# Window attention with token-major output, row sums from a ones column, and bias matmuls in 64-column tiles

## What is computed

```python
x = x + conv_ref(ln_c(x))                 # window attention, with residual
t = tokens(x);  t = t + ffn(ln_t(t))      # experts, with residual

# conv_ref, per window of 49 tokens
qkv  = xw @ w_qkv.T + b_qkv
attn = einsum('qd,kd->qk', q, k) / sqrt(8) + bias + mask
p    = softmax(attn, axis=-1)
o    = einsum('qk,kd->qd', p, v)
out  = o @ w_proj.T + b_proj

# ffn
probs = softmax(x @ gate_w + gate_b); masked = top-2 of probs, divided by their sum
y = sum_e masked[e] * (gelu(x @ w1[e] + b1[e]) @ w2[e] + b2[e])
```

## Time and profile before

| | |
|---|---|
| median of 3 runs | 7468.48 us (7466.52 to 7471.74) |
| span of the profiled execution | 7472.1 us |
| PE busy | 7129.8 us, 95% |
| PEld busy | 5658.9 us, 76% |
| DVE busy | 5951.8 us, 80% |
| ACT busy | 4441.6 us, 59% |
| POOL busy | 2691.2 us, 36% |
| mean granted clock of TensorE | 0.986 |
| L417 POOL, normalise_p, x1024 | 1213.6 us, 1185 ns each |
| L675 DVE, row sums, x1024 | 779.5 us, 761 ns each |
| L677 DVE, reciprocal, x1024 | 233.4 us, 228 ns each |
| L926 PE, transpose_p, x6144 | 854.3 us |
| L945 PE, attend, x24576 | 561.7 us |
| L954 PE, project, x3584 | 383.0 us |

### The profile page before, as it was taken

One profiled execution on the slowest core, in us unless ns is written; L12 is line 12 of the kernel. 1 busy time (PEld: TensorE's weight loads), 2 busy tenths in 40 slices (PEclk: granted clock), 3 DMA queues, 4 the chain that ended last, 5 costly groups with the idle time before them and its releaser, 6 DMA issues.

```text
span 7472.1 us, 236413 instructions
## 1 busy us (share of the span) xinstructions
PE 7129.8 (95%) x87040; PEld 5658.9 (76%) x87040; DVE 5951.8 (80%) x17441; ACT 4441.6 (59%) x8959; POOL 2691.2 (36%) x1799
## 2 busy tenths in 40 slices
PE   5999999999999999999999999999999999999998
PEld 4777777777777777777777777777777777777777
DVE  6788778888788887878787788787888778887886
ACT  4566655665566655656565566655665566655664
POOL 3333333333333333333333333333333333333332
PEclk9999999999999999999999999999999999999999
DMA  1111111111111111111111111111111111111110
GB/s 49 35 32 35 33 34 32 34 34 34 32 34 35 33 33 34 34 33 34 33 34 33 34 32 34 33 34 32 35 33 34 32 34 35 34 32 34 34 33 18
DMA packets 168131, 250.97 MB, mean 34 GB/s; under 512 B 44272, under 2 KB 129008, under 8 KB 166768
## 3 DMA queue, kind: packets, MB, share of 16 engines
q1 hardware_dynamic: 166896, 234.60, 11.0%
HBM read 80.28 MB, written 38.54 MB: 16 GB/s over the span
## 4 chain that ended last, share of the span: by engine, by line
PE 52%; issue 27%; POOL 13%; DVE 4%; ACT 2%; SPq 1%; POOLq 0%; DMA 0%; DVEq 0%
PE ps_f L1010 18%; PE ps_t L926 10%; PE ps_o L945 7%; PE ps_s L916 4%; POOL rstd L399 4%; POOL rstd L383 3%; PE ps_f L954 3%; PE ps_f L1007 3%; PE ps_s L907 3%; ACT pt_sb L498 2%; POOL xn L393 2%; POOL xn L388 2%; POOL p_sb L417 2%; PE ps_f L865 1%; DVE stat L691 1%
## 5 line engine op out<-in xcount | busy, mean ns | idle before, releaser
L417 POOL TENSOR_TENSOR p_sb<-p_sb,s_rec 113x588 f32<-113x588 f32 x1024 | 1213.6, 1185 | 3244.9 <-DVE s_rec L677 3244.9
L1010 PE MATMUL ps_f<-w_sb,g_sb 128*112 128x96 f32 x18432 | 1963.7, 261 | 0.0
L1010 PEld LDWEIGHTS ps_f<-w_sb,g_sb 128*112 128x112 f32 x18432 | 1916.3, 178 | 0.0
L483 ACT ACTIVATE g_sb<-ps_f 128x392 f32<-128x392 f32 x3072 | 1524.3, 497 | 287.8 <-PE ps_f L859 217.7
L494 ACT ACTIVATE p_sb<-s_sub 113x588 f32<-113x588 f32 x1024 | 723.3, 706 | 1612.2 <-DVE s_sub L665 1612.2
L857 PE MATMUL ps_f<-x_hi,w_hi 128*128 128x392 f16 x3072 | 1040.7, 339 | 117.7 <-issue 103.5
L663 DVE TENSOR_REDUCE s_max<-ps_s 113x12 f32<-113x588 f32 x1024 | 770.8, 753 | 412.1 <-PE ps_s L916 405.6
L858 PE MATMUL ps_f<-x_lo,w_hi 128*128 128x392 f16 x3072 | 1038.3, 338 | 0.0
L859 PE MATMUL ps_f<-x_hi,w_lo 128*128 128x392 f16 x3072 | 1036.9, 338 | 0.0
L675 DVE TENSOR_REDUCE s_sum<-p_sb 113x12 f32<-113x588 f32 x1024 | 779.5, 761 | 199.7 <-ACT p_sb L494 161.9
L926 PE MATMUL ps_t<-ident,p_sb 113*113 113x113 f32 x6144 | 854.3, 275 | 49.9 <-POOL p_sb L417 49.9
(11 more groups left out here) (114 smaller groups left out, 10867.8 us busy)
## 6 DMA issues: line engine op xcount, KB each, us to landing
k_st<-qk_hi SPq DMA_DIRECT2D x768, 49.0 KB, 2.0
q_st<-qk_hi SPq DMA_DIRECT2D x768, 49.0 KB, 2.0
xr<-x SPq DMA_DIRECT2D x224, 139.1 KB
out<-xr SPq DMA_DIRECT2D x224, 139.1 KB
xa<-x SPq DMA_DIRECT2D x224, 136.5 KB
k_st<-qk_lo SPq DMA_DIRECT2D x384, 49.0 KB, 2.0
q_st<-qk_lo SPq DMA_DIRECT2D x384, 49.0 KB, 2.0
xa<-x SPq DMA_DIRECT2D x224, 10.5 KB
```

What stands on the lines that cost most here:

```text
L417: nc.gpsimd.tensor_tensor(p, p, s_rec[:, :].unsqueeze(2).broadcast_to([SPAN, HEADS, WW]), ALU.mult).then_inc(pnorm_done, 1)
L483: nc.scalar.activation(g_sb[:, chunk, half * STRIP:(half + 1) * STRIP], h_bank[k % 3][:, 0:STRIP], ACT.Gelu, scale=1.0 / WSCALE).then_inc( ...
L1010: ins = T.matmul(y[:, k * C:(k + 1) * C], g_sb[:, e * CPE + c, j * LANES:(j + 1) * LANES], w2_sb[:, e * CPE + c, :], start=False, stop=(c ...
```

## The change

Probabilities are no longer divided before the product with the values. `v_bd` gets, for each head, a ninth column of ones (`VW` = 9, so 18 columns for two heads instead of 32), and the product's ninth column is the row sum. `attend` now takes the transposed probabilities as weights (49 columns) and `v_bd` as the moving operand (18 columns). Its output is token-major in two 64-column tiles. VectorE's new `normalise_o` takes the reciprocal of the sums and multiplies 96 columns, from PSUM to `o_tok`. The new `turn_o` is one f32 transpose for each pair (weights `o_tok`, moving a permutation matrix `turn`), and `save_o` copies four pairs at once, two copies per unit instead of eight. `o_sb` has one block and `project` 7 matmuls. `sums` and `normalise_p` are gone. The bias matmuls are issued as two 64-column tiles, and q times k alternates between the tiles. `s_sub` has two buffers. The orders on TensorE, ScalarE and VectorE are rearranged. The diff, cut to its core:

```diff
-COMBINES_AT = ((0,), (1,), (2,), (3, 4), (5,), (6,), (), (7,))
+VW = HD + 1
+OTW = 2 * WW
+O0 = 4 * OTW + 12
+        o_heads = ps_o[0:SPAN, O0:O0 + HEADS * VW].rearrange("p (h z) -> p h z", z=VW)
+        o_turned = ps_o[0:C, 0:4 * OTW]
# GpSimd: normalise_p and its calls removed; two memsets of v_bd's ones columns added in the setup
# ScalarE
-            def save_o(a, n):
+            def save_o(a, half):
+                act.wait_ge(turn_done, at(a, N_O, 4 * half + 4))
+                dst = o_sb[0:C, :].rearrange("p (c h r) -> p c h r", c=W, h=2)[:, :, half, :]
+                nc.scalar.activation(dst.rearrange("p c (n q) -> p c n q", n=4),
+                                     o_turned.rearrange("p (n c q) -> p c n q", n=4, c=W),
                                      ACT.Copy).then_inc(o_saved, 1)
             def attention(a, b):
                 exps(a, 0)
                 for n in range(8):
+                    if n == 7 and b is not None:
+                        qk_high(b, 0)
+                    copy_pt(a, n)
                     if n < 7:
                         exps(a, n + 1)
-                    if n == 7 and b is not None:
-                        qk_high(b, 0)
-                    if n:
-                        save_o(a, n - 1)
-                    if n == 7 and b is not None:
-                        qk_high(b, 1)
-                    copy_pt(a, n)
-                    if n == T1_AT and b is not None:
-                        x1_high(b)
+                    if n == 4:
+                        save_o(a, 0)
+                        if b is not None:
+                            x1_high(b)
+                if b is not None:
+                    qk_high(b, 1)
+                save_o(a, 1)
                 if b is not None:
                     qk_high(b, 2)
-                save_o(a, 7)
-                if b is not None:
                     v_copies(b)
# VectorE
-            def sums(a, n):
-                dve.wait_ge(exp_done, at(a, N_S, n + 1))
-                if n or not first(a):
-                    dve.wait_ge(pnorm_done, at(a, N_S, n))
-                V.tensor_reduce(s_sum[:, :], p_sb[0:SPAN, n % 2, :, 0:WW], AX.X, ALU.add).then_inc(sum_done, 1)
-                dve.wait_ge(sum_done, at(a, N_S, n + 1))
-                V.reciprocal(s_rec[:, :], s_sum[:, :]).then_inc(rec_done, 1)
+            def normalise_o(a, n):
+                dve.wait_ge(o_done, at(a, N_O, n + 1))
+                V.reciprocal(s_rec[:, :], o_heads[:, :, HD]).then_inc(rec_done, 1)
+                dve.wait_ge(rec_done, at(a, N_O, n + 1))
+                if n >= 2 or not first(a):
+                    dve.wait_ge(turn_done, at(a, N_O, n - 1))
+                V.tensor_tensor(o_tok[:, n % 2, :].rearrange("p (h d) -> p h d", d=HD), o_heads[:, :, 0:HD],
+                                s_rec[:, :].unsqueeze(2).broadcast_to([SPAN, HEADS, HD]), ALU.mult
+                                ).then_inc(onorm_done, 1)
             def attention(a, b, f=None, u=None):
                 for n in range(8):
-                    sums(a, n)
+                    if f is not None and n:
+                        combine(f, u, n)
                     if n < 7:
                         softmax_pair(a, n + 1)
-                    if f is not None:
-                        for g in COMBINES_AT[n]:
-                            combine(f, u, g)
+                    if f is not None and n == 0:
+                        combine(f, u, 0)
+                    if n:
+                        normalise_o(a, n - 1)
+                    if n == 7 and b is not None:
+                        qk_low(b, 0)
                     if b is not None:
                         x1_low(b, X1_LOW_AT[n])
+                normalise_o(a, 7)
                 if b is not None:
-                    qk_low(b, 0)
                     qk_low(b, 1)
# TensorE
+                s3 = ps_s[:, 0:HEADS * NB].rearrange("p (h k) -> p h k", k=NB)
+                blocks = ((slice(0, NB), slice(0, NB)), (slice(NB, SPAN), slice(NB, SPAN)))
                 for h0, h1 in ((0, 8), (8, 12)):
-                    T.matmul(s3[:, h0:h1, 0:WW], sel16[:, :], bias16[:, variant, h0 * WW:h1 * WW],
-                             start=True, stop=False, skip_group_check=True)
+                    for rows, cols in blocks:
+                        T.matmul(s3[rows, h0:h1, 0:WW], sel16[:, cols], bias16[:, variant, h0 * WW:h1 * WW],
+                                 start=True, stop=False, skip_group_check=True)
# q times k: the loop over g now stands outside the loop over s
             def attend(a, n):
+                    pe.wait_ge(onorm_done, at(a, N_O, n))
+                if n == 4:
+                    pe.wait_ge(o_saved, at(a, N_OT, 1))
+                for p in range(PAIRS):
+                    for s in range(2):
+                        win = half * NW + wr + s
+                        ins = T.matmul(ps_o[NB * s:NB * s + WW, O0 + p * 2 * VW:O0 + (p + 1) * 2 * VW],
+                                       pt_sb[0:SPAN, p, s * WW:(s + 1) * WW], v_bd[0:SPAN, win * PAIRS + p, :],
                                        start=True, stop=True, skip_group_check=True)
+            def turn_o(a, n):
+                pe.wait_ge(onorm_done, at(a, N_O, n + 1))
+                o0 = (n % 4) * OTW
+                T.transpose(ps_o[0:C, o0:o0 + SPAN], o_tok[:, n % 2, :], turn[:, :]).then_inc(turn_done, 1)
# project: one matmul for each of the 7 columns, no loop over blk
             def attention(a, b, f=None):
-                for n in range(9):
+                for n in range(8):
                     if n < 7:
                         scores(a, n + 1)
-                    for g in groups:
-                        experts(f, g)
-                    if n == T1_AT and b is not None:
-                        transpose1(b)
-                    if n >= 7 and b is not None:
-                        qk(b, 2 * (n - 7))
                     if n:
                         attend(a, n - 1)
                     if n == 7 and b is not None:
-                        qk(b, 1)
-                    if n < 8:
-                        transpose_p(a, n)
+                        qk(b, 0)
+                    transpose_p(a, n)
+                    if n == T1_AT and b is not None:
+                        transpose1(b)
+                    for g in groups:
+                        experts(f, g)
+                    if n:
+                        turn_o(a, n - 1)
                 if b is not None:
-                    values(b, (0,))
+                    qk(b, 1)
+                attend(a, 7)
+                if b is not None:
+                    values(b)
+                turn_o(a, 7)
+                if b is not None:
+                    qk(b, 2)
                 project(a)
-                if b is not None:
-                    values(b, (1,))
                 if f is not None:
                     experts(f, 8)
                 transpose2(a, b)
```

More of the change, by code:

```diff
@@ L127 @@
          ("rel", HEADS * WW), ("lr", HEADS * WW), ("ul", HEADS * WW), ("sel", SPAN), ("selB", SPAN))
-N_CONST = 5
+N_CONST = 6
 def build(nc, x, packed, w2, wp, consts, out):
@@ L377, in _ @@
             nc.gpsimd.memset(p_sb[:, :, :, :], 0.0).then_inc(s_zero, 1)
+            for odd in range(2):
+                pool.wait_ge(s_zero, 3 + odd)
+                nc.gpsimd.memset(v_bd[NB * odd:NB * odd + WW, :, VW * odd + HD:VW * (odd + 1)], 1.0
+                                 ).then_inc(s_zero, 1)
             def norm1(a):
@@ L410, in gate_exp @@
                                         ).then_inc(gexp_done, 1)
[L412 to L418, removed]
             def prologue():
@@ L501, in copy_pt @@
                     ACT.Copy).then_inc(pt_saved, 1)
-            def save_o(a, n):
-                half, wr = n // 4, 2 * (n % 4)
-                act.wait_ge(o_done, at(a, N_O, n + 1))
-                if n == 0 and not first(a):
+            def save_o(a, half):
+                act.wait_ge(turn_done, at(a, N_O, 4 * half + 4))
+                if half == 0 and not first(a):
                     act.wait_ge(proj_done, at(a, N_PROJ))
-                dst = o_sb[0:C, :, :].rearrange("p b (c h r) -> p b c h r", c=W, h=2)
-                nc.scalar.activation(dst[:, :, :, half, W * wr:W * (wr + 2)],
-                                     ps_o[0:C, 0:4 * WW].rearrange("p (b c r) -> p b c r", b=2, c=W),
+                dst = o_sb[0:C, :].rearrange("p (c h r) -> p c h r", c=W, h=2)[:, :, half, :]
+                nc.scalar.activation(dst.rearrange("p c (n q) -> p c n q", n=4),
+                                     o_turned.rearrange("p (n c q) -> p c n q", n=4, c=W),
                                      ACT.Copy).then_inc(o_saved, 1)
@@ L904, in scores @@
                 variant = 1 if half == 1 and a[1] % UPI == UPI - 1 else 0
-                s3 = ps_s[0:SPAN, 0:HEADS * NB].rearrange("p (h k) -> p h k", k=NB)
+                s3 = ps_s[:, 0:HEADS * NB].rearrange("p (h k) -> p h k", k=NB)
```

(27 more changed lines are left out.)

70 lines of the change are left out of this document (32 added, 38 removed).

## The result

| | before | after |
|---|---|---|
| median | 7468.53 us | 7630.09 us (7625.72 to 7630.84, 4 runs) |
| ratio | | 1.0214 (1.0199 to 1.0228) |
| span of the profiled execution | 7472.1 us | 7623.5 us |
| mean granted clock | 0.986 | 0.960 |

The change makes the kernel 2.1% slower. I had forecast 7612 us, with 7440 to 7740 as the range.

A forecast was written before the change was run, and what follows sets the result against it. TensorE, 95% busy, was taken to bound the kernel, so its savings show unless a wait replaces them. 7468.5 + 52 (chain) - 4 (prologue and setup) + 95 (clock) = 7611.5, say 7612 us; range 7440 to 7740.

The forecast's parts named there:

- The iteration: One attention iteration on TensorE: 3.91 us before, 3.95 after, +0.04, with attend rounds at 0.045 us.
- Rival 2: In attend: rounds cheap at 0.030 us, all on the path; 7434 with the falls, 7339 without. Chance 0.14.
- rival 4: In attend: load and move don't overlap, rounds at 0.063 us, 7828 in all. Chance 0.08.
- The first stretch: TensorE from scores of pair 0 to the seventh transpose: -0.16 us per step, with iteration 0 at -0.53.
- The tail: Seventh transpose to transpose2: normalise_o heads VectorE's queue, transpose2 starts at 11.34 instead of 10.77, +0.57 us; TensorE waits 1.88.
- the third stretch: From transpose2 to the next unit's scores, 14.35 us before: left as it is, no change counted.
- The clock: TensorE's new wait before transpose2 lets the clock fall in half of the steps, 1.5 us each: +95 us.
- Nothing is made up: On the hidden layer, TensorE and ScalarE's Gelu run equally fast, so a slow stretch's loss, 1.5 us, counts in full.
- Rival 1: At the tail: VectorE is late, but the clock holds through the 1.88 us wait: 7517. Chance 0.25.
- I expect falls: At transpose2: clock falls expected, since waits of 0.77 and 0.68 us in the last unit were enough for one.
- Prologue and end: The prologue, bound by the softmax chain, saves about 5 us; the larger setup costs 1: -4 us.
- Rival 3: At the tail: VectorE not late, residual starts once project is seen; transpose2 at 10.83, -0.10 us per step, 7452. Chance 0.08.

The follow-up runs named there:

- fill8: Changed kernel plus eight f32 matmuls that nobody reads, put between experts(8) and transpose2 where TensorE waits: 7520.36 us, ratio 1.0069 to the kernel before.
- proj2: Changed kernel with every projection matmul issued twice, 14 instead of 7: 7539.98 us, ratio 1.0095 to the kernel before.
- wait_half_b: Kernel before plus one memset of scratch memory in VectorE's residual, so that TensorE waits before transpose2: 7599.33 us, ratio 1.0175.
- ln1: Changed kernel with VectorE's ln1_stats moved from the tail into attention iterations 1 to 3: 7469.38 us, ratio 1.0000 to the kernel before.
- wait: Kernel before plus two memsets of scratch memory in VectorE's residual, so that TensorE waits before transpose2: 7836.80 us, ratio 1.0492.
- five_turns_b: On ln1 with half of values back behind project: one turn of expert group 7 moved into group 8. 7317.96 us, ratio 0.9802 to the kernel before.
- qkorder: Changed kernel with the old loop order of q times k, all of one tile, then the other: 7628.19 us, measured once.

## Why the prediction was right, step by step

**The iteration.** Forecast 3.95 us, measured 3.91. Five rows, in the kernel after:

```profile
3021.16 0.44 PE L918 MATMUL ps_s<-bias,sel 128*64 128x392 f16 x4
3021.44 0.43 PE L928 MATMUL ps_s<-k_bd,q_st 128*49 128x196 f16 x6
3021.70 0.69 PE L955 MATMUL ps_o<-v_bd,pt_sb 113*49 113x18 f32 x24
3022.32 0.85 PE L938 MATMUL ps_t<-ident,p_sb 113*113 113x113 f32 x6
...
3025.07 0.45 PE L918 MATMUL ps_s<-bias,sel 128*64 128x392 f16 x4
```

`attend`'s last record takes 0.20 us on average (L955, 198 ns), so eleven rounds span 0.69 - 0.20 = 0.49: 0.0445 a round, against 0.045 forecast from L1010's load of 112 columns. Rival 2 (0.030) and rival 4 (0.063) are out. A round takes as long as the old round of three 32-column tiles (0.045), though it moves 18 columns instead of 49, so `attend` costs more because it has 12 rounds instead of 8: its records span 0.69 us instead of 0.55. That the loaded columns set the pace now fits the numbers: 0.0445 us for 49 is 0.91 ns a column, 0.0975 for L1010's 112 is 0.87. No run varies the loaded columns alone. Of the rest, bias with q times k takes 0.54 us instead of the forecast 0.62, experts 1.88 instead of 1.92, and `turn_o` 0.19 instead of 0.10, since the gap stands between it and the bias.

**The first stretch.** -0.16 forecast, -0.22 measured: the wait for GpSimd at pair 0 is gone, and the wait for the first `save_o` is there in the kernel after (L511 shows 124 waits of PEld, 32.1 us in all, so 0.26 each). From the first bias to that of iteration 1 it is 6.01 us instead of 5.94. Iteration 5 then takes 4.15 us against 3.92 before, 0.23 more where I had 0.04 + 0.13, and the other five take what they took before, not 0.04 more. That gives 0.07 + 0.06 - 0.20 = -0.07 against the forecast, rounding aside.

**The tail.** Counted from `attend(6)`, forecast and measured: transposes of pair 7 from 1.30 and 1.20, `attend(7)` 2.81 and 2.71, `normalise_o(7)` 3.59 and 3.48, L693 6.96 and 6.83, `transpose2` 11.34 and 11.19, TensorE's wait 1.88 and 1.79. I had placed one start 0.1 us late, and all else follows it at the right distance. `normalise_o` takes 0.45 to the next start (forecast 0.44). So the two stretches came to +0.20 instead of +0.41. That the undisturbed step is still 0.31 longer is the third stretch, which I had left as it is "since nothing in them is edited": the change of tile width now comes before its end, at +0.10. The term should not have been nothing, since a bias in 64-column tiles behind a matmul of full width was part of the change. In sum 39 us instead of 52, because one error took half of the other away.

**The clock.** The mechanism and the place were right; the size was a guess between none and all, and both factors were off in opposite directions. I took half of the steps at 1.5 us, 95 us. There were 83 of 97 ordinary steps at 1.27 us, 105 us, and 21 of the 30 with a loop turn, and `fill8` gives 110 us for taking all of them away. That 95 comes near is luck. "Nothing is made up" was wrong too: the slow stretches of the 83 last 3.8 us on average, which at half the clock is 1.9 us of TensorE's time, and only 1.27 of it shows in the step. The mean clock of 0.972 that I named was too high; it is 0.960. Rival 1 (7517 with the clock held) comes close to what `fill8` measured, 7520.

The row on which I rested "I expect falls" carried less than I took from it. The waits of 0.77 and 0.68 us in the last unit follow on each other, and from 7418 to 7422 PE is busy in 2.55 of 4.00 us. In the dense steps of `proj2` and `wait_half_b` single waits of 0.73 and 0.93 us bring no fall.

**Prologue and end.** I forecast -4 us, with 5 us saved in the prologue. The prologue saved nothing: the first `transpose2` comes at 107.7 us instead of 107.5. What follows the start of the last one takes 50.3 instead of 51.6 us. Together -1.

**The sum.** The two traces span 7472.1 and 7623.5 us, 151.4 apart. The ordinary steps take 133 us more (0.31 x 97 = 30 for the chain, the rest falls), the 30 steps with a loop turn 19 (62.60 us on average instead of 61.95), and the two ends 1 less: 151. The medians lie 162 apart because the trace of the kernel before is of an execution longer than its median and that of the kernel after of the fastest of its four. Against the forecast of 143 us, the chain came out 13 us lower, the clock with what else the loop turns cost 18 higher, and the ends 3 higher.

**Rival 3** (VectorE not late) is refuted by L693, which follows L650 with no wait, and by `ln1`, where 0.48 us per step came back as soon as VectorE was free earlier.

**What stays open.** Why 104 units fall here and only 79 in `wait`, which has the longer wait, 2.03 against 1.79 us. The share of units with a fall rises steeply between 1.32 us (14 units) and 1.79 (104), with 0.93 (the 2 units that fell before too), 0.73, 0.55 and 0.22 (none) below. These waits stand in different kernels, so their length isn't the only thing that differs. The place in the loop body counts as well: of the 24 units without a fall in the kernel after, 21 are the last one before a loop turn (9) and the first behind it (12), while in `wait` it is 4 and 18, and 27 elsewhere. No run here separates the length of the wait from its place.

## What to carry to other kernels

Work taken off an engine that is 95% busy is worth little where another engine's chain ends last; there it mostly opens a wait (here 0.31 of 1.38 us were worth something). When an operation is given to an engine, look at what is queued behind it and who waits for that: here 0.45 us of `normalise_o` put itself ahead of 2.9 us of VectorE's work, and moving work that has no hurry (the next unit's statistics) out of that queue was worth 161 us. In this kernel a wait of TensorE near 2 us had a second price, the clock, and filling it took that price away even with useless matmuls. Real work from a place where TensorE is the bound is the better filling, since it also shortens that place (`five_turns_b`). And a change of tile width has its price at the border to the neighbouring stretch too, even where no line of that stretch is edited.

## What the runs showed of the hardware that I had not expected

Matmuls can start ahead of matmuls that stand before them in the program. In the iteration with a mask, which only the second tile adds, `attend` starts before q times k has started its last matmul (kernel after):

```profile
3017.45 0.33 PE L928 MATMUL ps_s<-k_bd,q_st 128*49 128x196 f16 x2
3017.53 0.23 PE L955 MATMUL ps_o<-v_bd,pt_sb 113*49 113x18 f32 x2
3017.62 0.25 PE L928 MATMUL ps_s<-k_bd,q_st 128*49 128x196 f16 x1
3017.62 0.27 PE L955 MATMUL ps_o<-v_bd,pt_sb 113*49 113x18 f32 x2
3017.70 0.25 PE L928 MATMUL ps_s<-k_bd,q_st 128*49 128x196 f16 x1
```

The Trainium skill (TensorE: Matmul & The Clock Gate, Part 3) says that matmuls keep program order in start and end. The rows differ from it in the starts; the ends in the profile are modelled and settle nothing. The rows don't name the tile of a record. That the early ones belong to the first tile, which has no mask to add, is my reading, and `qkorder` fits it: the order in which the two tiles' matmuls are written made no difference there.
